# A pairwise interaction kernel: the pairs with fields 0-3 computed with the batch on the partitions

## The reference: what is computed

```
e   = stack([tbl_f[ids[:, f]] for f in range(32)], axis=1)      # 1024 x 32 x 64
kp  = einsum('bpj,ipj->bpi', e[:, ROW], kernel)                 # 64x64 matrix per pair
z   = sum(kp * e[:, COL], axis=-1)                              # 1024 x 496
h   = concatenate([z, dense_ctx], axis=1)                       # 1024 x 512
h   = maximum(h @ W_top1 + b_top1, 0)                           # 512
h   = maximum(h @ W_top2 + b_top2, 0)                           # 256
y   = h @ W_top3                                                # 1024 x 1
```

## Time and profile before

| | |
|---|---|
| median of 3 runs | 454.15 us |
| the profiled execution's own time | 454.88 us |
| its span | 453.1 us |
| PE busy | 436.7 us (96%) |
| VectorE busy | 288.9 us (64%) |
| GpSimd busy | 242.4 us (54%) |
| ScalarE busy | 52.4 us (12%) |
| share of the chain of waits: PE / GpSimd / "issue" | 88% / 6% / 3% |

### The profile page before, as it was taken

The page is one execution under the profiler, slowest core; times in us unless marked ns, Lnnn a source line. Parts: engine busy times, 40 slices in busy tenths (PEclk is TensorE's granted clock), DMA queues, the critical chain, the costliest instruction groups (busy, mean ns, idle before and its releaser), DMA issues.

```text
span 453.1 us, 8090 instructions
## 1 busy us (share of the span) xinstructions
PE 436.7 (96%) x3428; PEld 266.1 (59%) x3428; DVE 288.9 (64%) x253; ACT 52.4 (12%) x79; POOL 242.4 (54%) x262
## 2 busy tenths in 40 slices
PE   8768899999999999999999999999999999999996
PEld 8655555666656666666565666665656666644442
DVE  0043767888768677777686778886887888860000
ACT  1000201011102000102020001111200020001122
POOL 6777777777777777777777777777300000000000
PEclk9998999999999999999999999999999999999999
DMA  2354358211111111111111111111000000000000
GB/s 67 100 135 132 102 160 319 61 26 28 28 28 29 27 29 29 28 27 29 26 30 28 26 28 28 28 28 29 18 1 1 1 1 1 1 1 1 0 1 0
DMA packets 11211, 18.83 MB, mean 42 GB/s; under 512 B 4836, under 2 KB 5160, under 8 KB 10920
## 3 DMA queue, kind: packets, MB, share of 16 engines
q0 software_dynamic: 8192, 8.40, 9.2%
q1 hardware_dynamic: 2984, 9.91, 6.8%
HBM read 18.29 MB, written 0.00 MB: 40 GB/s over the span
## 4 chain that ended last, share of the span: by engine, by line
PE 88%; POOL 6%; issue 3%; DMA 1%; DVE 1%; ACT 0%; DVEq 0%
PE u_ps L348 46%; PE z_ps L367 25%; POOL nat L208 6%; PE u_ps L386 6%; PE t_ps L331 4%; PE u_ps L355 3%; PE u_ps L408 3%; DMA nat<-tbl,ids_sb 1%; DVE prod L305 1%; DMA ids_sb<-ids 0%; PE u_ps L414 0%; ACT k_sb L283 0%; DVEq L137 0%; DVE y_sb L313 0%; DVEq L301 0%
## 5 line engine op out<-in xcount | busy, mean ns | idle before, releaser
L305 DVE TENSOR_TENSOR prod<-u_ps,rows 128x1024 f32<-128x1024 f32 x240 | 278.3, 1217 | 112.1 <-PE u_ps L348 112.0
L208 POOL DMA_INDIRECT nat<-tbl,ids_sb x256 | 241.7, 944 | 79.4 <-issue 76.8
L348 PE MATMUL u_ps<-rows,k_sb 64*128 64x256 f32 x1920 | 228.6, 386 | 4.6 <-issue 2.6
L348 PEld LDWEIGHTS u_ps<-rows,k_sb 64*128 64x128 f32 x1920 | 181.2, 187 | 77.2 <-DVE prod L305 48.7
L367 PE MATMUL z_ps<-prod,sel 128*32 128x512 f32 x992 | 119.5, 598 | 0.0
L367 PEld LDWEIGHTS z_ps<-prod,sel 128*32 128x32 f32 x992 | 25.8, 109 | 52.8 <-issue 38.4
L242 ACT ACTIVATE rows<-t_ps 128x512 f32<-128x512 f32 (+1 forms) x40 | 20.5, 512 | 275.3 <-PE t_ps L331 275.3
L313 DVE COPY y_sb<-u_ps 1x256 f32<-1x256 f32 x2 | 0.8, 424 | 44.8 <-PE u_ps L414 44.8
L331 PE MATMUL t_ps<-ident,nat 128*128 128x128 f32 x128 | 22.7, 290 | 6.3 <-DMA nat<-tbl,ids_sb 6.2
L386 PE MATMUL u_ps<-zT,w_sb 128*128 128x512 f32 x64 | 27.7, 594 | 0.0
L331 PEld LDWEIGHTS t_ps<-ident,nat 128*128 128x128 f32 x128 | 13.3, 141 | 18.8 <-issue 10.8
(11 more groups left out here) (14 smaller groups left out, 7.3 us busy)
## 6 DMA issues: line engine op xcount, KB each, us to landing
nat<-tbl,ids_sb POOLq DMA_INDIRECT x256, 2.5
k_sb<-kern SPq DMA_DIRECT2D x3, 768.0 KB, 4.2
k_sb<-kern SPq DMA_DIRECT2D x2, 640.0 KB, 3.9
k_sb<-kern SPq DMA_DIRECT2D x1, 1152.0 KB, 7.0
k_sb<-kern SPq DMA_DIRECT2D x2, 512.0 KB, 3.5
w_sb<-w SPq DMA_DIRECT2D x1, 1024.0 KB
k_sb<-kern SPq DMA_DIRECT2D x1, 896.0 KB
k_sb<-kern SPq DMA_DIRECT2D x3, 256.0 KB, 2.9
```

The lines of the kernel that those rows point to most:

```text
L208: pool.indirect_dma_start(nat[:, m % RING, n, h * EMBED:(h + 1) * EMBED], None, tables[f], bass.IndirectOffsetOnAxis(ids_sb[:, col:col + 1 ...
L305: op = nc.vector.tensor_tensor(to, u, by.unsqueeze(1).to_broadcast([P, 2, 2, SIZE]), ALU.mult)
L348: op = nc.tensor.matmul(u[:, h, :], k_sb[part, d, side, :], rows[part, tile, cols], start=True, stop=True)
```

## The change

Fields 0 to 3 are tiles 0 and 1. Their pairs with fields 4 to 31 were 14 of the 62 doubles of a block, and are now 14 *passes* (`interact_pass`). A pass takes one half of a block's batch (128 samples) and two tiles: the looked-up rows are the weights, the pairs' matrices stream through. So the result has the samples on the partitions and, along the free dimension, 16 pairs of 64 numbers. VectorE multiplies it by rows 0-3 as they were gathered, not transposed (`nat01`, kept for two blocks). The 64 products of a pair now lie along the free dimension, and their sums are not PE's: ScalarE makes eight of a pass's sixteen, one instruction each, with `accum_out`; VectorE makes the other eight in one reduction. They go to `z_nat`, 112 columns beside the 16 dense ones, which a DMA brings there. Two transposes of PE (`fold`) a block turn `z_nat` into the fourth row of `zT`.

The other 48 doubles are added up as before, in 24 quads a block: 16 of them (`g == 0`) as they were, 8 with eight matmuls of 256 columns, since both sides now share one row of `zT`. The MLP's weights lie in `rows`, in columns of block 0, and are loaded after block 0. Before a block's tile 0, from block 2 on, GpSimd waits for the passes of two blocks earlier.

The order comes from a class `Plan`. Passes stand behind every fourth double, one or two at a time, when their tiles are there. ScalarE's sums are dealt out three to a piece, at least two pieces behind their pass. A *piece* is a double or a pass.

```diff
-URING, PRING, RING = 3, 8, 8
+URING, PRING, CRING, RING, LANES = 3, 8, 3, 8, 8
...
-DOUBLE, TURN, TRANSPOSE, FILL = 1.3, 0.17, 0.13, 0.23
+DOUBLE, QUAD, CHANGE, TURN, TRANSPOSE, FILL = 0.86, 0.87, 0.34, 0.2, 0.12, 0.23
...
+        self.append((b, d, None), here)
+        self.add_sums(3, 2)
+        if n % BURST == BURST - 1:
+            self.add_pass()
+            if len(self.open) < 2:
+                self.add_pass()
...
+            def add_along(b, j, first, end):
+                tile, s = pass_of(j)
+                if first == 0:
+                    act.wait_ge(prod_ready, AT[b, None, j] + 1)
+                for x in range(first, end):
+                    t, field = x // 4, x % 4
+                    row = pass_row(tile + t, 0, field)
+                    of = pass_prod[:, (b * NP + j) % CRING, 0, t, field * EMBED:(field + 1) * EMBED]
+                    op = nc.scalar.activation(of, of, ACT.Copy, accum_out=z_nat[:, b % 2, s, row:row + 1])
+                if end == SUMS:
+                    op.then_inc(pass_summed, 1)
...
+            def multiply_pass(n, b, j):
+                u, k = u_ps[:, n % URING], b * NP + j
+                dve.wait_ge(u_ready, n + 1)
+                if k >= CRING:
+                    dve.wait_ge(pass_summed, k - CRING + 1)
+                    dve.wait_ge(pass_reduced, k - CRING + 1)
+                by = nat01[:, b % 2, pass_of(j)[1]].rearrange("p t n -> p (t n)").unsqueeze(1).unsqueeze(1)
+                nc.vector.tensor_tensor(pass_prod[:, k % CRING], u, by.to_broadcast([P, 2, 2, SIZE]), ALU.mult).then_inc(prod_ready, 1)
+
+            def reduce_pass(n, b, j):
+                tile, s = pass_of(j)
+                dve.wait_ge(prod_ready, n + 1)
+                if j == 0 and b >= 2:
+                    dve.wait_ge(z_transposed, b - 1)
+                to = z_nat[:, b % 2, s, 0:P - DENSE].rearrange("p (t h f) -> p t h f", h=2, f=4)[:, tile - 2:tile, 1, :]
+                of = pass_prod[:, (b * NP + j) % CRING, 1].rearrange("p t (f n) -> p t f n", f=4)
+                nc.vector.tensor_reduce(to, of, mybir.AxisListType.X, ALU.add).then_inc(pass_reduced, 1)
+
+            for n, (b, d, j) in enumerate(PLAN.order):
+                if d is not None:
+                    multiply_double(n, b, d)
+                else:
+                    multiply_pass(n, b, j)
+                if n > 0 and PLAN.order[n - 1][2] is not None:
+                    reduce_pass(n - 1, PLAN.order[n - 1][0], PLAN.order[n - 1][2])
...
+            def interact_pass(n, b, j):
+                first, s = pass_of(j)
+                at = b * SIZE + s * P
+                if n >= URING:
+                    pe.wait_ge(prod_ready, n - URING + 1)
+                pe.wait_ge(rows_ready, b * TILES + first + 2)
+                for t in range(2):
+                    k = K_ORDER.index(((first + t, 0), (first + t, 1)))
+                    for h in range(2):
+                        part = slice(EMBED * h, EMBED * (h + 1))
+                        op = nc.tensor.matmul(u_ps[:, n % URING, h, t, :], rows[part, first + t, at:at + P],
+                                              k_sb[part, k].rearrange("p s n -> p (s n)"), start=True, stop=True)
...
+                else:
+                    for side in range(2):
+                        row = 16 * side + 2 * slot
+                        for k in range(4):
+                            op = nc.tensor.matmul(z_ps[32 * k:32 * k + 32, 0, :], sel[:, 30 - row:62 - row],
+                                                  prod[:, (a + k // 2) % PRING, k % 2, side], start=slot == side == 0, stop=last and side == 1)
```

More of the change, by code:

```diff
@@ L78, in lane_count @@
 def lane_count(m):
-    return 32 * SUBS * (m // RING + 1)
-K_FIRST = [min(d for d in range(ND) if tile_of(d) == tile) for tile in range(2, TILES)] + [ND]
+    return 32 * SUBS * (m // LANES + 1)
+K_FIRST = [min(d for d, double in enumerate(K_ORDER) if (double[1] or double)[0] == tile) for tile in range(2, TILES)] + [NK]
 K_AFTER_TILE = [max(0, tile - 3) for tile in range(2, TILES)]
 START, TILE_TIME, LANDING = 3.0, 5.0, 2.4
-DOUBLE, TURN, TRANSPOSE, FILL = 1.3, 0.17, 0.13, 0.23
[L91 to L128, removed]
@@ L134, in tower @@
+PLAN = Plan()
+AT = {what: n for n, what in enumerate(PLAN.order)}
+PIECES = len(PLAN.order)
+assert PIECES == len(AT) == BLOCKS * (ND + NP)
 def tower(nc, ids, tables, kern, dense, w1, b1, w2, b2, w3, out):
@@ new lines, in zT_evacuate @@
+            def zT_evacuate(b):
+                act.wait_ge(z_transposed, b + 1)
+                nc.scalar.activation(zT[:, ZROWS - 1, cols_of(b)], t_ps[:, 0].rearrange("p n c -> p (n c)"), ACT.Copy).then_inc(zT_out, 1)
+            act.wait_ge(z_zero, 1)
+            for n, (b, d, j) in enumerate(PLAN.order):
+                for m, count in PLAN.before[n]:
+                    rows_out(m, count)
+                if d is not None and d + 3 < ND and DOUBLES[d + 3][1] is None:
+                    gather_by_self(b, d + 3)
+                for which in PLAN.sums[n]:
+                    add_along(*which)
+                for m, count in PLAN.behind[n]:
@@ L309, in _ @@
-                op.then_inc(prod_ready, 1)
+                    by = rows[:, one[1]:two[1] + 1:two[1] - one[1], cols_of(b)]
+                    nc.vector.tensor_tensor(to, u, by.unsqueeze(1).to_broadcast([P, 2, 2, SIZE]), ALU.mult).then_inc(prod_ready, 1)
+                else:
+                    dve.wait_ge(by_self_ready, 2 * sum(e is not None and DOUBLES[e][1] is None for _, e, _ in PLAN.order[:n + 1]))
+                    nc.vector.tensor_tensor(to, u, by_self.rearrange("p s b n -> p b s n"), ALU.mult).then_inc(prod_ready, 1)
@@ L347, in interact @@
                             part = slice(EMBED * h, EMBED * (h + 1))
-                            op = nc.tensor.matmul(u[:, h, :], k_sb[part, d, side, :], rows[part, tile, cols], start=True, stop=True)
+                            op = nc.tensor.matmul(u[:, h, :], k_sb[part, k_of(d), side, :], rows[part, tile, cols_of(b)], start=True, stop=True)
                     else:
@@ L372, in _ @@
             pe.wait_ge(sel_ready, 2)
[L373 to L381 removed]
+            k_here, tiles, folds = 1, 0, 0
+            for n, (b, d, j) in enumerate(PLAN.order):
+                for m, count in PLAN.before[n]:
+                    fill(n, PLAN.fill[m])
+                    transpose(m, count, folds)
+                    tiles += count
+                needed = tile_of(d) if d is not None else pass_of(j)[0] + 1
+                while k_here < needed:
+                    k_here += 1
+                    pe.wait_ge(k_in[k_here], 16)
+                if d is not None:
+                    interact(n, b, d)
+                else:
+                    interact_pass(n, b, j)
+                for m, count in PLAN.behind[n]:
+                    transpose(m, count, folds)
+                    tiles += count
+                for quad in PLAN.quads[n]:
+                    add_up(quad)
+                if PLAN.folded[n] is not None:
+                    fold(PLAN.folded[n], tiles)
+                    folds += 1
+            for quad in range(BLOCKS * QUADS - BURST // 2, BLOCKS * QUADS):
+                add_up(quad)
             def h1_product(n):
@@ L396, in _ @@
             pe.wait_ge(z_out, BLOCKS * ZGROUPS)
[L397 to L398 removed]
+            pe.wait_ge(zT_out, BLOCKS)
             for n in range(4, 8):
```

284 lines of the change are left out of this document (181 added, 103 removed).

## The result

| | before | after |
|---|---|---|
| median, same chips | 454.7 us (15 runs) | 457.33 us (15 runs) |
| ratio to before | | 1.0039, 95% interval 1.0021 to 1.0058 |
| profiled execution / its span | 454.88 / 453.1 us | 456.16 / 454.1 us |
| the MLP's first matmul starts at | 406.68 us | 407.71 us |

The kernel became slower by 0.39%, about 1.8 us (0.95 to 2.6). Two of the 15 runs after, of 857 and 1479 us, are slow ones that nothing here explains, and the ratio is taken from the fast runs alone. Forecast were 453.5 us and a change of -0.6: the time lies inside the range, but on the other side of no change. The two profiled executions are 1.0 us apart where the adding up ends; the budget further down is made against them.

What follows compares the result with a forecast made beforehand. The prediction took PE, running without gaps, to bound the kernel. Its terms, -29.4 + 3.6 + 4.4 + 20.8 = -0.6 us, led to a forecast of 453.5 us, with a range of 443 to 465.

Steps and rivals of the forecast that it cites:

- Removed, -29.4: PE's chain: 28 fewer quads in adding up (24.1 us) and 16 fewer groups of quads (5.3) save 29.4 us.
- PE's gains, +3.6: Work added on PE: quads of eight matmuls +0.6, folds +1.5, pairs of tiles transposed just before use +1.5 us.
- halved quads: Adding up on PE: 32 quads of eight 256-column matmuls cost 0.88 us each instead of 0.86, +0.6 in all.
- the rival of short matmuls: Adding up on PE: a quad of eight matmuls costs 1.1 to 1.7 us, giving 460 to 480; chance 0.06.
- two pair copies: Block 1: two pairs of tiles transposed just before their double, copy not hidden, 0.74 us each, +1.5 in all.
- The start, +4.4: While gathers come slowly: three pieces and a group of quads are put off until PE is full, +4.4 us.
- VectorE's waits, +20.8: Bursts with passes: reductions delay products, so PE waits 0.63 us for one pass, 0.93 for two; +20.8 after deductions.
- two groups of five: Bursts excused from waits: five two-pass bursts following one without a pass (-3.1 us), five with a transpose inside (-3.5).
- ScalarE's sums: ScalarE's 448 copies with running sum: 0.35 us each taken, hidden in PE's time.
- The rival of ScalarE as the bound: Stretches holding the passes: from 0.60 us a sum ScalarE has no room, copies come late, some 465; chance 0.15.
- PE not held by VectorE: Rival for bursts: lag hides in PE's queue and reductions are cheap, so 433 to 445 us; chance 0.17.
- VectorE as the bound: Rival for bursts: longer reductions make VectorE's work exceed PE's, +7 to +15, so 461 to 468 us; chance 0.10.

Runs made afterwards that it cites:

- e1: The changed kernel without VectorE's 56 reductions and the waits for them: 441.58 us, ratio 0.970.
- e7: The changed kernel with two passes laid behind each of the program's first and third doubles, where PE waits for gathers: 453.53 us, ratio 0.9949.
- e2: The changed kernel without ScalarE's 448 sums and the waits for them: 456.81 us, ratio 1.0028.
- e3: The changed kernel with all 16 sums of a pass made by ScalarE and no reduction on VectorE: 444.96 us, ratio 0.977.
- e10: As e9, but ScalarE makes 12 of a pass's 16 sums and VectorE's reduction makes four: 439.98 us, ratio 0.966.
- e6: The kernel before the change with 63 added reductions, one behind each burst's first product on VectorE: 455.25 us, ratio 0.9987.
- e4: The changed kernel with each reduction moved one instruction forward on VectorE, ahead of the burst's first product: 444.17 us, ratio 0.976.
- e9: The changed kernel with both the edit of e4 and the edit of e7: 441.73 us, ratio 0.969.

## Why the prediction was right and wrong, point by point

**Removed, -29.4, and PE's gains, +3.6.** The chains of before and of e1 are nearly all PE from tile 7's transpose to the MLP, so their pieces can be added up. Adding up takes 113.0 us (122 quads) before and 59.2 + 29.6 = 88.8 (all 96) in e1: -24.2. The prediction had for this stretch 28 quads (-24.1), 16 entries (-2.1), the group put off from the start (+1.85) and 0.6 for the halved quads: -23.7. So halved quads cost 0.2 us in all and not 0.6 (two at 1.86, where whole ones are 1.85); the rival of short matmuls is out. The folds are four times 0.37, as taken, and the two pair copies are 0.82 each for 0.74.

PE's busy time fell by 11.8 us and not by the 26 forecast. Of the difference 6.4 is `fill`: 204 records and 26.6 us, against 148 and 20.2 before, in time in which PE waits for gathers anyway. The rest was not split.

**The start, +4.4.** The MLP of e1 starts 14.0 us before that of the kernel before. Of that -24.1 - 5.3 + 0.2 + 3.0 = -26.2 are the terms above. In e1's chain 15 single passes stand at 1.00, ten pairs at 2.13, four pairs at 1.93, and four odd ones, against 0.86 and 1.72: 2.1 + 4.1 + 0.8 + 0.6 = 7.6 us that VectorE costs even without reductions. What remains is 26.2 - 7.6 - 14.0 = 4.6 for the start, where 4.4 was predicted. This 4.6 is a remainder and holds what the other terms have wrong, and also when the gathers happened to land: counted from tile 7's transposes (46.40 before, 45.63 in e1) it is 5.4. e7, which takes out a part of it, gained 2.95.

**VectorE's waits, +20.8: the step that failed, by its size.** By the runs it is 22.6: 15.0 that come with the reductions (after less e1) and 7.6 that stay without them. The forecast of -0.6 became +1.0 in the profiles by +1.8 here, +0.2 at the start and -0.4 for the halved quads. That the terms now add up to +1.0 is no test of them, since the 4.6 and the 15.0 are differences of the same three profiles.

The mechanism was as predicted: the reduction behind the first product, three buffers, the fifth and sixth piece. The part that comes with the reductions came out nearly as forecast. The prediction's count, 35 bursts less its two groups of five, leaves 25 that pay; 25 was also measured (e1), at 0.59 for the 0.63 taken: 15.0, with the 0.2 before the first quads, for 15.8. What was too small is the rest, what a burst longer than four pieces costs by VectorE's products alone. The prediction had for it 20.8 - 15.8 = 5.0, for second passes at 0.30. In e1 it is 7.6: two passes cost 0.41, and a single one 0.14, which no term held.

Inside a burst two errors met. The wait of a first pass is shorter than taken: it would have started at 183.20 + 3.65 = 186.85 and started at 187.32, 0.47 for 0.63, since a reduction holds VectorE for 0.59 and the lag to PE is 0.04 to 0.05 (187.27 to 187.32), not 0.10. But after the wait PE doesn't go on as it did: the first piece takes 1.13, not 0.86, so 0.27 more, which no term held either. One pass: 195.55 + 1.13 - (191.43 + 3.65 + 0.86) = 0.74 for 0.63. Two: 189.58 - (183.20 + 3.65 + 1.72) = 1.01 for 0.93. Times 17 and 18 that is 30.8 for 27.4; against it the deductions are 8.2 and not 6.6. The row for the restart was there: a first double is 1.06 in the earlier trace rows, 1.13 in the earlier trace rows, and the prediction had 0.20 of it as the price of entering a stretch, but not as the price of every wait.

That the time fell inside the range says little. The range, 443 to 465, is 22 us wide, and the direction hung on a difference of under 2 us between terms of 26 and 27.

**ScalarE's sums.** 0.24 us each where 0.35 was taken, and hidden (e2). The rival of ScalarE as the bound is out for 8 sums a pass; with 16 the copies that stand behind sums cost 4.3 us (e3).

**PE not held by VectorE, VectorE as the bound.** The first is what e1 and e10 show, at 441.58 and 439.98, inside that rival's 433 to 445, but only once the reductions are gone or moved. The second is out, by e6 and e4. The rule of the Trainium skill in "VectorE: DVE Perf Modes", section "The DRAIN you can't avoid", read as in the prediction, would have the product behind a reduction wait for a flush after the reduction's end; by that page's 266 ns this is an estimate of 1.09 us from one start to the next. It started 0.59 after the reduction did, 0.09 before its end (186.05, the reduction from 185.46 for 0.68). The section adds that a next operation that is not held starts earlier; with that the trace agrees, whatever makes the page count an operation as held, which no run here tests.

**The last 0.8 us.** The profiles are 1.0 apart, the ratio says 1.8 with 0.95 to 2.6. Tile 7's last gather landed at 46.35 in the profile before, at 45.26 in e7's and at 46.05 in e9's, and its transposes stand at 45.09 in that of the kernel after. So single executions differ by a microsecond or so before PE is full, and a pair of profiles can't be held to less. Counted from tile 7's transposes to the MLP the two profiles are 360.28 and 362.62 long, 2.3 apart. The 1.8 lies between the two counts, and no further cost is needed for it.

That three buffers set the limit is read from the kernel's waits and from e6; a kernel with a fourth `u_ps` buffer, which by the same count would let PE go on to a fifth piece, wasn't tried.

## What to carry to other kernels

An instruction on an engine with time to spare is paid by its place: count how many pieces the producer can be ahead (here three), and put extra work where the consumer's queue is empty, ahead of a burst's first piece, not behind it. The same 56 reductions cost 15.0 us in one place and 2.3 one instruction earlier. When you price a wait, add the restart of the engine that waited, and price the start of a program, where data come in slowly, as its own stage: here the new kind of work had been kept out of it, and four passes put there gave 2.95 us (only 1.0 in the profiles once the reductions had moved).

## What the runs showed of the hardware

- A float32 piece of PE (8 records) takes 0.86 us in a row, 1.06 to 1.09 (chain of waits) behind matmuls of another shape, and 1.13 to 1.15 behind a wait for another engine.
- VectorE's operations overlap: 1.217 long at a pace of 1.155, and a reduction of 0.676 at 0.59.
- ScalarE's running sum adds a record of 0.188 us that lies partly under its neighbours: 0.24 us from sum to sum.
- Eight float32 matmuls of 256 columns in four column tiles cost as much as four of 512 (1.86 for two such quads, 1.85 for the others).
